# A gated cross-attention and mixture-of-experts layer: the first half's routing and 18 scatters moved into the attention loop, weight pieces split two a turn, and their scaling moved from GpSimd to ScalarE

## The reference

```
x = x + tanh(g_xattn) * Attention(layernorm(x), ctx, ctx, mask)          # 32 x 128 rows of 128, 16 heads of 8
f = layernorm(x)
shared = mean over 2 shared experts of gelu(f @ sW1 + sb1) @ sW2 + sb2
gates = f @ rW + rb ;  top 2 of 8 experts, softmax over the two
moe = sum over the two chosen experts of w * (gelu(f @ W1[e] + b1[e]) @ W2[e] + b2[e])
out = x + tanh(g_ffn) * (shared + moe)
```

## Time and profile before

| what | value |
|---|---|
| median of 3 executions | 484.74 us (484.67 to 486.93) |
| profiled execution, from first to last instruction | 524.9 us |
| busy in it: PE, DVE, ACT, POOL | 415.9, 397.8, 340.8, 315.9 us |
| mean granted TensorE clock | 0.955 of full speed |

### The profile page before, as it was taken

One profiled execution on the slowest core, in us unless ns is written; L12 is line 12 of the kernel. 1 busy time (PEld: TensorE's weight loads), 2 busy tenths in 40 slices (PEclk: granted clock), 3 DMA queues, 4 the chain that ended last, 5 costly groups with the idle time before them and its releaser, 6 DMA issues.

```text
span 524.9 us, 13531 instructions
## 1 busy us (share of the span) xinstructions
PE 415.9 (79%) x4611; PEld 297.2 (57%) x4611; DVE 397.8 (76%) x983; ACT 340.8 (65%) x674; POOL 315.9 (60%) x382
## 2 busy tenths in 40 slices
PE   0377979879998989776784989898999989998930
PEld 0245767758776877554341433344878777776720
DVE  7696769868778778987774896494888768886795
ACT  0536857657787877665663876495677567765743
POOL 9151524494987889598876376650466656666550
PEclk9998989899999999988997989999999999999985
DMA  8767863442333534540011011113122222244119
GB/s 226 223 197 202 223 146 80 103 101 75 78 87 84 114 82 142 178 164 17 26 51 45 27 41 41 47 36 81 36 78 77 70 72 86 67 132 138 58 44 280
DMA packets 71753, 53.19 MB, mean 101 GB/s; under 512 B 7473, under 2 KB 63548, under 8 KB 71688
## 3 DMA queue, kind: packets, MB, share of 16 engines
q1 hardware_dynamic: 64608, 42.96, 30.2%
q0 software_dynamic: 4544, 8.44, 4.6%
q10 hardware_dynamic: 2536, 0.94, 0.7%
HBM read 29.38 MB, written 24.33 MB: 102 GB/s over the span
## 4 chain that ended last, share of the span: by engine, by line
PE 25%; DVE 8%; issue 5%; another core or an unknown queue 5%; ACT 4%; POOL 2%; DMA 1%; ACTq 0%; DVEq 0%; POOLq 0%
PE pAtt L1123 9%; PE pE L1111 4%; PE pS L1111 4%; DVE HH L1490 3%; PE pAtt L1061 2%; PE pMix L1101 2%; PE pS L999 2%; ACT H L767 1%; POOL yd L622 1%; PE pE L999 1%; DVE HH L1486 1%; ACT G L803 1%; DMA YY<-yd 1%; DVE t_X L1543 1%
## 5 line engine op out<-in xcount | busy, mean ns | idle before, releaser
L622 POOL DMA_INDIRECT yd<-Y,XR x78 | 85.0, 1089 | 72.5 <-DVE Y L1529 45.4
L1234 DVE TENSOR_REDUCE t_MX<-pS 128x4 f32<-128x512 f32 x128 | 86.4, 682 | 24.0 <-PE pS L861 22.4
L720 ACT ACTIVATE PT<-pE,t_mbias,t_scl 128x512 f32<-128x512 f32 x128 | 97.1, 788 | 6.6 <-PE pE L861 6.4
L597 POOL DMA_INDIRECT xs<-t_STG,t_pos x64 | 64.2, 1002 | 36.5 <-issue 15.4
L1123 PE MATMUL pAtt<-t_W2h,HR 128*128 x624 | 65.3, 219 | 6.8 <-issue 5.5
L803 ACT ACTIVATE G<-pS,t_b1T,t_inv 128x256 f32<-128x256 f32 x78 | 40.0, 569 | 43.6 <-remote 39.3
L1490 DVE SCALAR_TENSOR_TENSOR HH<-H,t_sc,HH 128x512 f16<-128x512 f32 x64 | 48.4, 761 | 21.6 <-ACT HH L772 14.7
L1521 DVE SCALAR_TENSOR_TENSOR HR<-G,t_sc,HR 128x512 f16<-128x512 f32 x78 | 58.6, 751 | 2.8
L1123 PE MATMUL pAtt<-t_W2l,HR 128*128 x312 | 56.4, 219 | 3.4 <-issue 3.4
L1123 PEld LDWEIGHTS pAtt<-t_W2h,HR 128*128 128x128 f16 x624 | 50.0, 97 | 12.6 <-issue 10.9
L861 PE MATMUL pE<-t_Q,t_K 128*128 128x128 f16 x512 | 51.6, 225 | 5.8 <-DMA t_Q<-MPT 4.8
(11 more groups left out here) (276 smaller groups left out, 1044.5 us busy)
## 6 DMA issues: line engine op xcount, KB each, us to landing
xs<-t_padrow SPq DMA_DIRECT2D x10, 516.0 KB, 5.3
XR<-xs SPq DMA_DIRECT2D x39, 129.0 KB
scr<-QKS SPq DMA_DIRECT2D x16, 256.0 KB, 2.2
t_Q<-scr SPq DMA_DIRECT2D x16, 256.0 KB
t_K<-scr SPq DMA_DIRECT2D x32, 128.0 KB
t_STG<-in_W SPq DMA_DIRECT2D x7, 512.0 KB, 6.4
YY<-yd SPq DMA_DIRECT2D x14, 256.0 KB, 5.8
t_X<-in_x SPq DMA_DIRECT2D x4, 512.0 KB, 6.5
```

The source lines that it names most:

```text
L597: g.indirect_dma_start(k.xs, bass.IndirectOffsetOnAxis(ap=pos[:, n:n + 1], axis=0), k.PAY[:, n, :], None).then_inc(h.di[q], 16)
L622: g.indirect_dma_start(k.yd, bass.IndirectOffsetOnAxis(ap=XR[u][:, q, D:ROW], axis=0), Y[u][:, q, :], None, bounds_check=2 * T - 1, oob_is ...
L720: act.activation(PT[:, m % NPT], pE[g % 2][:], ACT.Exp, bias=k.mbias[:, bt:bt + 1], scale=k.scl[:, bt:bt + 1]).then_inc(s.exp, 1)
L1234: v.tensor_reduce(out=MX[:, n % G // 4, m % 2, m // 2::2], in_=pS[n % 2][:], axis=AX_X, op=ALU.max).then_inc(s.max, 1)
```

## The change

- `SPLITS` has another order. `units_of(t)` gives one piece in turn 5, two in each of turns 6 to 14, one in turn 15.
- ScalarE scales each piece (`scale_weights`, in groups 2 and 5 of the turn), GpSimd waits for it (`s.ws1`) and does only the cast and the subtraction.
- Payloads and gates of pairs 0 to 7 move from turns 9 to 16 to turns 7 to 14; `RSTD` has seven groups in place of five.
- The choice of the first half moves from turns 17 and 18 to turns 14 and 15, its prefix counts from turn 18 to turn 15 (into pMix in place of pS), its slots to turns 15 and 16, with one more copy (G2).
- GpSimd issues 18 of the 64 scatters inside the loop: 2, 5, 5, 6 in turns 16 to 19 (`SCATTERED`), ahead of the turn's payloads. The payloads of the last two pairs follow these, and then come the other scatters. The index of each half is written by an iota of its own.
- The padding DMAs go one a turn in turns 5 to 14. `first_scales` moves from group 5 to group 1 of turn 5.

```diff
-    SPLIT = LAG + 3
-    FIRST_W2 = 4
-    UBODIES = END - SPLIT - 1
+    SPLIT = LAG + 2
+    FIRST_W2 = split_done(1, 0) - 1
+    FIRST_ROWS = NP // 2 - 1
+    SCATTERED = {16: 2, 17: 5, 18: 5, 19: 6}
+    PACED = 4
+    SECOND_FROM = 22
...
-        at = lambda j: min(max(j, 0) * UNITS // UBODIES, UNITS)
+        at = lambda j: min(max(2 * j - 1, 0), UNITS)
...
-        if not 9 <= t < END:
-            return ()
-        return (t - 9,) if t <= 16 else (2 * t - 26, 2 * t - 25)
+        if FIRST_ROWS <= t < FIRST_ROWS + NP // 2:
+            return (t - FIRST_ROWS,)
+        return (2 * t - 26, 2 * t - 25) if NP < t < END else ()
...
-    RSTD = {8: (0, 4), 12: (4, 4), 16: (8, 4), 18: (12, 2), 20: (14, 2)}
+    RSTD = {6: (0, 2), 8: (2, 2), 10: (4, 2), 12: (6, 2), 16: (8, 4), 18: (12, 2), 20: (14, 2)}
...
-                g.tensor_scalar(stg, stg, k.sc[:, sc:sc + 1], None, ALU.mult).then_inc(s.wh, 1)
-                g.wait_ge(s.wh, 2 * n + 1)
+                g.wait_ge(s.ws1, n + 1)
                 g.tensor_copy(hi[:, cols], stg).then_inc(s.wh, 1)
...
+                if t == NP - 1:
+                    first_index(0)
+                    g.wait_ge(k.s_empty, 16 * NE)
+                for _ in range(SCATTERED.get(t, 0)):
+                    next(scattered)
                 for p in normalised_in(t + 1):
                     payload(p)
...
-                    wait(g, h.lo, order - FREE)
+                    wait(g, h.lo, order - after)
...
+            def scale_weights(n):
+
+                which, e = SPLITS[n]
+                act.wait_ge(s.ws, which + 1)
+                if which and 5 <= e < 9:
+                    act.wait_ge(s.T, e + 8)
+                stg, sc = weights_read(which, e), (3, 5)[which]
+                act.activation(stg, stg, ACT.Copy, scale=k.sc[:, sc:sc + 1]).then_inc(s.ws1, 1)
...
+                    if g in (2, 5) and g // 3 < len(units_of(t)):
+                        scale_weights(units_of(t)[g // 3])
...
-                    if t == END - 3 and g < G - 1:
+                    if t == NP - 2 and g > 4 or t == NP - 1 and g != 4 or t >= NP:
                         next(first, None)
-                    if t == END - 2 and g > 1 or t == END - 1:
-                        next(first, None)
+                    if t >= NP:
                         next(first, None)
```

102 lines of the change are left out of this document (59 added, 43 removed).

## The result

The changed kernel takes 500.8 us (median of 4 runs, 499.5 to 501.4) beside 485.6 us for the kernel before: a ratio of 1.0306, 95% interval 1.0279 to 1.0333. It is slower by 15 us; 488.4 was forecast, and the range ended at 495.

The account below looks back on a forecast made before the run. No engine alone bounds a turn: it is a ring of PE, ScalarE and VectorE. The terms 5.1 - 1.8 + 2.0 + 1.6 + 4.0 - 4.2 - 1.0 - 2.0 = +3.7 us on 484.7 gave 488.4 us, range 476 to 495.

Parts of the forecast that it names:

- Scaling, relief and seven groups: Attention turns: ScalarE's scalings +5.1 us, GpSimd losing its scalings -1.8, seven groups of inverse deviations in place of five +2.0.
- the gapless stretch: ScalarE's work without idle time from XCT to 161.6 us; one scaling a turn there costs 9 x 0.5 = 4.5 us.
- The payload behind the scaling: PE's wait for payload rows in turns 7 to 14, behind the piece ScalarE scales last: put at nothing.
- GpSimd relieved: Turns 6 to 14: 18 scalings fewer on GpSimd speed small VectorE instructions before MPT, -1.8 us (bounds 0 and -5.4).
- Choice and slots: Turns 14 to 16: choice about +1.6 us and slots +4.0 on VectorE, bounds together +1 and +8.
- Turns 17 to 19: Attention's end: GpSimd's six payloads and ten scatters take 25.6 us, the loop ends earlier, -4.2 us (bounds 0 and -8).
- last payloads: Shared stage: PE's wait for the last payloads, now behind six scatters in place of 8, -1.0 us (bounds 0 and -2.3).
- scatters gone: Shared stage: 18 scatters leave it, -2.0 us, between none and -5.
- Rival (c): Attention turns: second scaling not covered either, ScalarE bounds at 11.7 us a turn and more; +9.3, 494.0 us; chance 0.10.

Follow-up runs that it names:

- the two kernels of the last set: Changed kernel with both pieces scaled at group 2: 493.5 us, ratio 1.0182; the same with choice, slots and scatters late as well: 484.3 us, ratio 0.999.

## Why the prediction was wrong

By ratios on the 485 us sort, the 15 us are two things: the place of the second scaling, 1.0306 - 1.0182 = 0.0124, or 6.0 us; and choice, slots and scatters inside the loop, 1.0182 - 0.999 = 0.019, or 9.3 us (each uncertain by some 2.5 us). The rest of the change is -0.5 us, no difference.

- **Scaling, relief and seven groups (+5.1 - 1.8 + 2.0 = +5.3).** Measured +6.0 - 0.5 = +5.5 in the total. That this sum fits is in part luck. Right was that the scaling in the gapless stretch costs and the one ahead of MPT does not. Its price was not: forecast at 0.5 us a turn, it is 1.4 (8.4 us in six turns, by the kernel with both at group 2), of which half is found in slower shifts on VectorE and a sixth of the 9.0 us in PE's clock. How much of it is ScalarE's stretch and how much GpSimd's work beside the shifts is not told apart: no run of the changed kernel moves one without the other. The seven groups cost 5.6 us alone beside GpSimd's scalings, and nothing beside well placed ones. Turns 8 to 14 themselves grew by 9.0 us, more than the total shows.
- **The payload behind the scaling**, which I had put at nothing and named as a possible cost: right at nothing. PE's waits for payload rows add up to 1.5 us in turns 8 to 14, and with GpSimd's waits for the scaling removed these turns stayed within 1.2 us.
- **GpSimd relieved (-1.8).** In the changed kernel this relief did not come: the shifts, from which I had it, take 8.4 us in six turns for 7.4. I had counted 18 scalings taken out of turns 6 to 14, but before only 13 of the 20 stood there, and more casts and subtractions came in; and I priced how much GpSimd does, not when. With both scalings at group 2 the relief is there (4.1 us): in the kernel before VectorE is then busy 50.72 us in turns 8 to 14 for 54.13, and these turns are 0.6 us shorter (68.81 for 69.41). That this relief is what made the four groups free in the changed kernel is likely, but only argued.
- **Choice and slots (+5.6).** Right: 34.7 us become 40.0 in the windows from turn 14 to 17; 31.8 against 38.0 are the two kernels of the last set with late and with early choice, and 32.4 against 39.1 those without any scatter in the loop.
- **Turns 17 to 19 (-4.2), last payloads (-1.0), scatters gone (-2.0): this is the step that failed.** -7.2 us were to pay for choice and slots. Between the kernels with and without early choice and scatters (spans 491.1 and 480.5) the 10.6 us divide as +1.3 up to turn 14, +6.2 from 14 to 17, -1.2 from there to the last exponential (242.82 and 236.52), +4.7 to the first GELU (255.94 and 244.91), and -0.4 for all that follows. So up to the first GELU -1.2 + 4.7 = +3.5 for -4.2 - 1.0 = -5.2; and -0.6 (first to last GELU, 90.3 and 90.9) for -2.0. Three profiles divide the 3.5: from the copy of MPT of turn 17 to the first GELU the two kernels without scatters in the loop take 21.0 us with late and 18.8 with early choice, -2.2, and the changed kernel takes 24.7, so that the scatters in the loop cost some 5.8 (one profile each, and from two sorts of chip). I had the length of GpSimd's chain right, 25.4 us for 25.6, and held its start fast. It waits for the inverse deviations of turn 16, which stand on VectorE among the slots, and these wait for PE. The chain came 19 us later than before, 3 of them beyond the delay of the loop itself (16.2), and ten scatters in it, 12.6 us by my own sum, made it what PE waits for. Without them GpSimd had room: it waited 4.3 and 9.2 us for the next inverse deviations.

Rival (c), the second scaling not covered, comes nearest to the turns, with 11.7 us a turn where 13.1 were measured. None had the late end.

What stays open: what the early choice and the scatters each cost in the total on the faster sort of chip, where only both together were taken back; why the stages behind the attention take back what a shorter attention gains (three kernels ended the exponentials some 4 us earlier and were no faster); and what ScalarE's long waits are on the slower sort of chip.
